# Block 0 of a network of residual blocks on one core: one mask transfer a slot, two key buffers, one product to divide heads, the maxima's rows copied by ScalarE, a norm in one piece ahead of the keys

## The reference

```python
def _attn(q, k, v, mask):
    scores = jnp.einsum('bqhd,bkhd->bhqk', q, k) / np.float32(np.sqrt(HD))
    scores = jnp.where(mask[:, None, None, :], jnp.float32(-jnp.inf), scores)
    w = jax.nn.softmax(scores, axis=-1)
    return jnp.einsum('bhqk,bkhd->bqhd', w, v)
```

## Time and profile before

| | |
|---|---|
| median of 3 runs | 5856.54 us (5856.24 to 5871.77) |
| the profiled execution | 5850.62 us, span 5848.7 us |
| busy: TensorE, its weight load | 5394.6, 4270.3 us |
| busy: VectorE, ScalarE, GpSimd | 4044.0, 3144.3, 2240.2 us |
| mean granted clock of TensorE | 0.961 of full speed |
| block 0 | from about 60 to 2960 us of the span |

### The profile page before, as it was taken

How to read it: one execution, slowest core, us unless ns; L and a number is a source line. 1 busy time by engine, 2 the same in 40 slices (tenths; PEclk the granted TensorE clock), 3 DMA queues, 4 the chain that set the end, 5 groups by cost and what they waited for, 6 DMA issues and landing times.

```text
span 5848.7 us, 144909 instructions
## 1 busy us (share of the span) xinstructions
PE 5394.6 (92%) x57797; PEld 4270.3 (73%) x57797; DVE 4044.0 (69%) x8355; ACT 3144.3 (54%) x6405; POOL 2240.2 (38%) x2209
## 2 busy tenths in 40 slices
PE   5899999999999999999978999999699999989998
PEld 4667677676776766767645799998389889947984
DVE  3888887888888888888744377776556666644653
ACT  1566666766666667666644333434334334424764
POOL 4665665666666666666500000000011111075440
PEclk8999999999999999999988999999899999998998
DMA  2776776767767777677810011110100000030000
GB/s 63 118 124 100 122 116 108 122 110 117 120 110 120 112 114 123 103 124 116 119 51 20 22 33 33 38 37 13 41 12 12 17 17 12 12 121 11 2 1 26
DMA packets 440503, 408.12 MB, mean 70 GB/s; under 512 B 125576, under 2 KB 420947, under 8 KB 437787
## 3 DMA queue, kind: packets, MB, share of 16 engines
q1 hardware_dynamic: 439834, 398.85, 39.2%
HBM read 158.00 MB, written 0.46 MB: 27 GB/s over the span
## 4 chain that ended last, share of the span: by engine, by line
PE 61%; POOL 8%; DVE 7%; SPq 7%; issue 6%; DMA 5%; ACT 4%; POOLq 1%; DVEq 1%; ACTq 0%
PE psum L2248 10%; PE psum L2278 10%; PE psum L1575 5%; PE psum L1587 4%; PE psum L1561 4%; SPq L1475 3%; POOL slot_context L3547 3%; DMA l_ctx_v<-in_ctxV 3%; PE psum L1609 3%; PE psum L1723 3%; PE psum L1601 2%; PE psum L416 2%; SPq L1493 2%; PE psum L430 2%; DVE row_max L1940 2%
## 5 line engine op out<-in xcount | busy, mean ns | idle before, releaser
L1940 DVE TENSOR_REDUCE row_max<-psum 112x1 f32<-112x500 f32 x2304 | 1443.5, 670 | 187.4 <-PE psum L1575 172.6
L2067 ACT ACTIVATE weights<-psum 125x448 f32<-125x448 f32 x2304 | 1141.3, 541 | 521.7 <-PE psum L1561 515.2
L1575 PE MATMUL psum<-key_stack,query_stack 97*128 97x500 bf16 x2304 | 875.7, 381 | 107.9 <-DMA query_stack<-query_parts 47.9
L1561 PEld LDWEIGHTS psum<-query_stack,key_stack 121*128 121x128 bf16 x9216 | 654.6, 99 | 370.7 <-issue 184.4
L1561 PE MATMUL psum<-query_stack,key_stack 121*128 121x112 bf16 x9216 | 837.9, 213 | 33.5 <-ACT weights L2067 28.0
L2278 PE MATMUL psum<-l_ctx_v,l_weights 125*128 125x129 f32 x5376 | 638.6, 274 | 1.8 <-ACT l_u L2352 1.8
L2278 PEld LDWEIGHTS psum<-l_ctx_v,l_weights 125*128 125x128 f32 x5376 | 618.3, 191 | 2.5 <-issue 2.5
L1587 PE MATMUL psum<-weights,values 125*17 125x112 f32 x18432 | 554.9, 261 | 0.0
L1587 PEld LDWEIGHTS psum<-weights,values 125*17 125x17 f32 x18432 | 408.9, 97 | 144.8 <-issue 140.4
L2097 POOL TENSOR_TENSOR key_parts<-key_temp,key_parts 128x500 bf16<-128x500 f32 x288 | 327.2, 1136 | 421.5 <-ACT key_parts L1970 421.5
L2087 POOL TENSOR_TENSOR key_temp<-key_temp,rope_sin 128x500 f32<-128x500 f32 x288 | 360.5, 1252 | 282.2 <-DVE key_temp L1821 282.2
(11 more groups left out here) (549 smaller groups left out, 10227.5 us busy)
## 6 DMA issues: line engine op xcount, KB each, us to landing
key_stack<-key_parts SPq DMA_DIRECT2D x1728, 125.0 KB, 4.6
ctx_t<-in_ctxT SPq DMA_DIRECT2D x96, 750.0 KB
l_ctx_v<-in_ctxV SPq DMA_DIRECT2D x32, 750.0 KB
query_stack<-query_parts SPq DMA_DIRECT2D x576, 28.0 KB, 3.4
l_ctx_t<-in_ctxT SPq DMA_DIRECT2D x16, 750.0 KB
slot_context<-in_ctxV SPq DMA_DIRECT2D x16, 750.0 KB
key_stack<-ctx_mask_rows SPq DMA_DIRECT2D x576, 3.9 KB
sm_w<-in_sm_w SPq DMA_DIRECT2D x3, 2048.0 KB
```

Source lines behind the costliest of these rows:

```text
L1561: mm = e.matmul(self.k.psum[:, h, (p % 4) * QC:(p % 4 + 1) * QC], ks[:, at:at + 128], q[:, p * QC:(p + 1) * QC])
L1575: e.matmul(self.k.psum[:, 2 + n % 2, 0:500], q[0:ROWS_MAX, p * QC:p * QC + 128], ks[0:ROWS_MAX, p, c * 500:(c + 1) * 500]).then_inc(self.m ...
L1940: e.tensor_reduce(self.largest[:, i % PAIRS, i // PAIRS:i // PAIRS + 1], k.psum[0:QC, 2 + i % 2, 0:500], AX.X, ALU.max, negate=True).then_ ...
L2067: e.activation(half(self.p[kt % RING_P], h), self.k.psum[0:KN, h, 0:HALF], ACT.Exp).then_inc(self.exped.sem, 1)
```

## The change

1. The mask of the context is held as one row of 1500 for each batch (16 partitions) instead of six of 250, and SP stacks it with one transfer a slot instead of six.
2. `key_temp` becomes two buffers, taken in turn, so VectorE waits for the last part of the block before the last.
3. The transposed sums' pieces are placed 8 columns lower for odd ones, so that all heads lie 32 columns apart and `divide` needs one product instead of four.
4. The rows are copied by ScalarE (`rows_scalar`), at the top of step 11, ahead of the exponentials of that step.
5. GpSimd applies both halves of a norm in one step, and does so ahead of its query and key work of that step.

```diff
-            self.mask_rows = sb("ctx_mask_rows", [6 * B, L // 6], BF16)[:, :]
+            self.mask_rows = sb("ctx_mask_rows", [B, L], BF16)[:, :]
...
-            for n in range(6):
-                e.dma_start(dst[ROWS:ROWS + 1, :, n * 250:(n + 1) * 250],
-                            self.mask_rows[6 * b + n:6 * b + n + 1, :].unsqueeze(1).broadcast_to(
-                                [1, PAIRS, 250])).then_inc(self.mask_stacked.sem, 16)
+            e.dma_start(dst[ROWS:ROWS + 1, :, :],
+                        self.mask_rows[b:b + 1, :].unsqueeze(1).broadcast_to([1, PAIRS, L])).then_inc(
+                            self.mask_stacked.sem, 16)
...
             for i in range(4):
-                tr = e.transpose(side.bank(*key)[0:S, i * 128:(i + 1) * 128], self.acc[:, i * S:(i + 1) * S],
-                                 k.ident[:, :])
+                at = i * 128 - 8 * (i % 2)
+                tr = e.transpose(side.bank(*key)[0:S, at:at + 128], self.acc[:, i * S:(i + 1) * S], k.ident[:, :])
...
-        for g in range(2):
-            for h2 in range(2):
-                v = blocks[:, g, 128 * h2:128 * (h2 + 1)].rearrange("p (j c) -> p j c", j=4)[:, :, 1 + 8 * h2:9 + 8 * h2]
-                m = 2 * g + h2
-                op = e.tensor_tensor(o[:, m * 32:(m + 1) * 32].rearrange("p (j d) -> p j d", j=4), v,
-                                     spread(inv[:, 4 * m:4 * m + 4], 8), ALU.mult)
-        op.then_inc(side.emptied(*key), 1)
+        e.tensor_tensor(o.rearrange("p (m d) -> p m d", d=8), bk.rearrange("p (m c) -> p m c", c=32)[:, :, 1:9],
+                        spread(inv, 8), ALU.mult).then_inc(side.emptied(*key), 1)
...
-            if (b, c) > (0, 0):
-                e.wait_ge(self.key_lo.sem, self.key_lo(b, c) - 1)
-            bk = side.bank(*key)[:, 0:500]
-            e.stream_shuffle(self.tm[:, 1, :], bk, OTHER_HALF).then_inc(self.key_turned.sem, 1)
+            if (b, c) > (0, 1):
+                e.wait_ge(self.key_lo.sem, self.key_lo(b, c) - 2)
+            bk, tm = side.bank(*key)[:, 0:500], self.tm[(3 * b + c) % 2]
+            e.stream_shuffle(tm[:, 1, :], bk, OTHER_HALF).then_inc(self.key_turned.sem, 1)
...
-    def rows_vector(self, e, b):
+    def rows_scalar(self, e, b):
...
-        e.tensor_copy(self.q_stack[b % 3][ROWS:ROWS_ALL, :].rearrange("r (p c) -> r p c", p=PAIRS),
-                      rows.unsqueeze(1).broadcast_to([1 + 3 * PAIRS, PAIRS, QC])).then_inc(self.side.emptied(*key), 1)
+        e.activation(self.q_stack[b % 3][ROWS:ROWS_ALL, :].rearrange("r (p c) -> r p c", p=PAIRS),
+                     rows.unsqueeze(1).broadcast_to([1 + 3 * PAIRS, PAIRS, QC]), ACT.Copy).then_inc(
+                         self.side.emptied(*key), 1)
...
         for s in self.slots():
             for kt in range(KT):
+                if 0 <= s + 1 < NS and kt == 11:
+                    self.rows_scalar(e, s + 1)
                 for h in range(2 if 0 <= s < NS else 0):
...
+                ph, t = s // BH, 12 * (s % BH) + kt
+                for name, at in T_NORM.items():
+                    layer = MLP_OF(ph) if name == "mlp" else NEXT_OF(ph)
+                    if layer is not None and t == at + 3:
+                        for h in range(2):
+                            self.norm_gpsimd(e, name, ph, layer, h)
                 if 0 <= s + 2 < NS:
                     self.query_gpsimd(e, s, kt)
                 self.key_gpsimd(e, s, kt)
-                ph, t = s // BH, 12 * (s % BH) + kt
-                for name, at in T_NORM.items():
-                    layer = MLP_OF(ph) if name == "mlp" else NEXT_OF(ph)
-                    if layer is not None and t - at - 3 in range(2):
-                        self.norm_gpsimd(e, name, ph, layer, t - at - 3)
```

More of the change, by code:

```diff
@@ L1290, in __init__ @@
             self.q_tmp = sb("query_block", [128, 2, QC])
-            self.tm = sb("key_temp", [128, 2, 500])
+            self.tm = [sb(f"key_temp{i}", [128, 2, 500]) for i in range(2)]
             self.ctx_t = [sb(f"ctx_t{i}", [128, L])[:, :] for i in range(2)]
@@ L1313, in __init__ @@
                 self.src_mask8 = k.sb(s2, "src_mask8", [1, T], U8)[:, :]
-                self.ctx_mask8 = k.sb(s2, "ctx_mask8", [6 * B, L // 6], U8)[:, :]
+                self.ctx_mask8 = k.sb(s2, "ctx_mask8", [B, L], U8)[:, :]
         self.tables_arrived = ev("l0_tables_arrived", step=112)
@@ L1328, in __init__ @@
         self.part_stacked = [ev(f"key_part{i}_stacked", NS * 3 // 2, step=16 * len(K_PARTS)) for i in range(2)]
-        self.mask_stacked = ev("key_mask_stacked", NS, step=96)
+        self.mask_stacked = ev("key_mask_stacked", NS, step=16)
         self.q_stacked = [ev(f"query_stack{i}_arrived", NS // 3, step=16 * len(Q_PARTS)) for i in range(3)]
@@ L1509, in sync @@
         e.dma_start(self.parity, dr["head_parity"]).then_inc(sem, 16)
-        e.dma_start(self.ctx_mask8, dr["ctx_mask"]).then_inc(sem, 16)
+        e.dma_start(self.ctx_mask8, dr["ctx_mask"].rearrange("(b n) c -> b (n c)", b=B)).then_inc(sem, 16)
         e.dma_start(self.bias[:, :, :], dr["l0_bias"]).then_inc(sem, 16)
@@ L1739, in phase_tensor @@
                 for m in range(4):
-                    tr = e.transpose(side.bank(*key)[0:S, m * 128:(m + 1) * 128], self.sacc[:, m * S:(m + 1) * S],
-                                     k.ident[:, :])
+                    at = m * 128 - 8 * (m % 2)
+                    tr = e.transpose(side.bank(*key)[0:S, at:at + 128], self.sacc[:, m * S:(m + 1) * S], k.ident[:, :])
                 tr.then_inc(side.filled, 1)
@@ L1817, in fixed_vector @@
             e.wait_ge(side.filled, side.at(*key))
-            if (b, c) > (0, 0):
-                e.wait_ge(self.key_lo.sem, self.key_lo(b, c) - 1)
-            bk = side.bank(*key)[:, 0:500]
-            e.stream_shuffle(self.tm[:, 1, :], bk, OTHER_HALF).then_inc(self.key_turned.sem, 1)
-            e.tensor_tensor(self.tm[:, 0, :], bk, self.cos[:, cols], ALU.mult).then_inc(side.emptied(*key), 1)
+            if (b, c) > (0, 1):
+                e.wait_ge(self.key_lo.sem, self.key_lo(b, c) - 2)
+            bk, tm = side.bank(*key)[:, 0:500], self.tm[(3 * b + c) % 2]
+            e.stream_shuffle(tm[:, 1, :], bk, OTHER_HALF).then_inc(self.key_turned.sem, 1)
+            e.tensor_tensor(tm[:, 0, :], bk, self.cos[:, cols], ALU.mult).then_inc(side.emptied(*key), 1)
         if 1 <= s <= NS and kt == 2:
@@ L1933, in vector @@
                     self.max_parts_vector(e, s + 1)
-                if 0 <= s + 1 < NS and kt == 11:
-                    self.rows_vector(e, s + 1)
                 if self.max_at(s, kt):
@@ L2074, in key_gpsimd @@
     def key_gpsimd(self, e, s, kt):
-        tm, side = self.tm, self.side
+        side = self.side
         for late in range(1, 4):
@@ L2083, in key_gpsimd @@
             b, c = at
-            part = self.k_part[(3 * b + c) % 2]
+            part, tm = self.k_part[(3 * b + c) % 2], self.tm[(3 * b + c) % 2]
             if late == 1:
```

9 lines of the change are left out of this document (4 added, 5 removed).

## The result

The changed kernel took 5882.96 us in the median against 5853.44 for the kernel before: 1.0047 times, 95% interval 1.0039 to 1.0054, some 27 us slower. The forecast was 5885. The experiments took it apart.

The account below looks back on a forecast made before the run. TensorE, busy 477.68 of 500 us, was taken as the bound. The terms summed to +31 us on the profiled 5850.62, so 5882, or 5887 as a median; the forecast was put at 5885, range 5840 to 5925.

Parts of the forecast that it names:

- Wait behind the MLP's norm: Step 9, eleven slots: GpSimd's norm delays the key and ScalarE's key copy, TensorE stands 4.2 each; +46 us.
- The clock behind it: TensorE's granted clock falls behind each of these eleven long waits, 2.0 us each; +22 us, bounds 0 to 37.
- The first rival: The wait is there, but TensorE's clock holds or other waits give it back: +9, 5865 us; chance 0.17.
- Self and cross norms and two buffers: Remainders 1 and 5: VectorE's 0.32 wait for the last key part goes, 0.33 in 22 places; -7 us.
- Rows on ScalarE: Rows' copy: -18 us from TensorE's waits behind remainders 2 to 4, +7 from 0.25 in 27 light slots.
- Mask: SP's five fewer issues a slot shorten TensorE's waits for queries: -15 us, and -5 for the clock.
- Divide: One product instead of four saves VectorE 0.4 in 184 places, hidden by TensorE; 5 us at best, no loss.
- Start: Ahead of the first self attention: +2 us for the masks' longer conversion, less 1 for the first slot's queries.
- The sum: All terms together: 46 + 22 + 7 + 1 - 7 - 18 - 15 - 5 = +31 us.
- The signs named in advance: Profile after: ScalarE's key copy and TensorE wait about 4 us eleven times, half clock behind, query waits 25 to 35, maxima's waits up.
- The third rival: ScalarE is not held behind the MLP's norm, as the roots come early enough: -37, 5820 us; chance 0.13.
- The second: TensorE's waits for queries go whole, all 47.9 us and eight stretches at lower clock: -11, 5846 us; chance 0.10.

Follow-up runs that it names:

- b_mask_only: The kernel before with one mask transfer a slot instead of six and nothing else changed: 5828.16 us, ratio 0.9960.
- a_norm_old: The changed kernel with the norm's part undone whole, every norm in halves behind the keys: 5829.34 us, ratio 0.9960.
- the first experiment: The changed kernel with the MLP's norm alone put behind the key again, half in step 9 and half in step 10: 5811.05 us.
- b_norm_only: The kernel before with only both halves of every norm in one step, ahead of the keys: 5975.25 us, ratio 1.0199.
- the half dose: The changed kernel with the first half of the MLP's norm ahead of the key and the second half behind it: 5853.4 us.

## Why the prediction was right, point by point

- **Wait behind the MLP's norm**, 46: right, and the mechanism was seen as forecast. One wait is 4.86 in slot 48, not 4.2. The norm and key took 6.43 against 6.38, and started 0.10 later behind the roots; the rows' copy pushes back by 0.10 more than the 0.82 I took; from the pair of exponentials to TensorE it is 0.69, not 0.49, as I counted no signal; and TensorE gets there 0.19 earlier. That is 0.64. Against the kernel without the hold it is 4.34 a time, 48 in all, since 0.58 of the step would be there by the rows' copy anyway.
- **The clock behind it**, 22: 23 by the account. The 2.0 for one were 2.1. The first rival, that the clock holds, falls.
- **Self and cross norms and two buffers**, -7: the buffer gave 9, by the very 0.33 named. That the norm ahead gives nothing by itself since VectorE's rotation is next was right too: 8.57 stays 8.57. The step that failed is that I costed it beside the kernel before: in company with ScalarE's copy it gives 22 us, because the copy makes ScalarE last there. Costing two buffers at nothing beyond the 7 left out that they are the condition of the norm's part: without them it costs 52 us more (117 against 65).
- **Rows on ScalarE**, -18 + 7: wrong by 39 us as a part alone (+28). The gain's places were right: the five steps behind remainder 2 to 4 are 0.36 to 0.49 shorter, and the 7.8 are gone. The cost was mis-placed and mis-sized: 0.58 in each light slot, not 0.25 (27 times, 16 us, not 7), and 1.05 in step 11 of 22 slots behind the self and cross norms, where ScalarE had a wait of 3.13 and thus no lead. Behind the cross norm half or less of that 1.05 stays by the end of the next slot's step 1 (8.73 to 9.08 against 8.57). Most of the error in the light slots can be named from the rows of slot 47. TensorE starts 0.69 behind the pair of exponentials (1608.20 to 1608.89), of which I counted 0.49 for the first, so 0.20 is left for the signal and not 0.1. The copy pushes back by 0.93 (1607.27 to 1608.20) and not 0.82. The prediction's own sum then gives 0.93 + 0.20 - 0.68 = 0.45. On top came 20 us of clock and 20 of waits for queries. Taken out of the changed kernel, though, the same part is worth -8 (error 9), which the forecast's -11 fits. Which term one calls wrong depends on the company in which it is measured.
- **Mask**, -15 - 5: -14 and -9 in block 0, -23 in all. The waits' part was right to a us or two, the list's 29.5 to 32.2 lie in the 25 to 35 named. In the last slot the lateness is gone as read: the second key block's issue starts at 2950.11, 0.02 behind its last part. The wait is not so simply the smaller of two numbers. It went from 2.91 to 1.52 in the changed kernel, 1.39 of the 1.6 to gain, but to 2.14 with the mask's part alone, 0.77 of them. SP's issues are not of one length either: the six of that key block took 3.88 in the kernel before, 4.34 and 5.05 in these two. SP and TensorE in the changed kernel, then TensorE in b_mask_only:

```profile
2947.11 0.70 SPq L1482 DMA_DIRECT2D key_stack<-ctx_mask_rows  x1
2950.11 4.34 SPq L1475 DMA_DIRECT2D key_stack<-key_parts  x6
```

```profile
2961.03 0.39 PE L1574 MATMUL psum<-key_stack,query_stack 97*128 97x500 bf16 x1 [1.52 <-DMA query_stack<-query_parts]
```

```profile
2905.96 0.38 PE L1574 MATMUL psum<-key_stack,query_stack 97*128 97x500 bf16 x1 [2.14 <-DMA query_stack<-query_parts]
```

- **Divide**, 0: not to be told from none.
- **Start**, +2 - 1: the masks' conversion takes 3.98 us against the 3.9 forecast, but the first scores of slot 0 come at 178.9 before and 178.0 after, and between 176.7 and 184.7 in the other kernels. No run here can tell a term of 1 us from none.
- **The sum.** With the norm's part taken out of the changed kernel and the other four put alone into the kernel before it is 73 - 22 - 9 + 28 - 23 - 3 = +44 against +27 measured. (With the norm's part put in alone too it would be 117 - 9 + 28 - 23 - 3 = +110: the parts don't add.) The 17 left over are by the medians no larger than their error, but the waits of block 0 (one execution each) show the same more clearly: -14, -2, +30 and +3.5 alone make +17.5, and the four together (a_norm_old) make -11. The wait for queries shows most of it: 47.9 before, 67.6 with the rows' copy alone, 29.5 with one mask transfer alone, and 30.5 with both and the others (a_norm_old). The same wait is 54.1 with the divide part alone, so it moves by some 6 by itself. That the copy delays ScalarE and so what SP waits for, and that SP has room for it with five issues fewer, is argued and not shown. So my two errors, 24 us of gain too little for the self and cross norms with the buffers and, with this, some 22 of cost too little for the rows, cancelled; the sum was right by its large terms and by that luck.
- **The signs named in advance.** All held: the maxima's waits, forecast up behind the rotations, are up there (0.56 to 0.79), though down in total, from 33.4 (53 times) in the same list of the kernel before to 23.5.
- The third rival (ScalarE not held) is out by the first experiment. The second (queries' waits go whole) is out: they went by a third.

The Trainium skill (VectorE: DVE Perf Modes, Mode 2×_1P) had been weighed for whether ScalarE would double on the 16-bit rows. The trace after answers for this shape: 896 bf16 columns take 905 ns on ScalarE, what the 0.82 ns a column of its fp32 rows gave (0.91), as against 618 on VectorE. There is no doubling; the page, which states the packing of VectorE, is not contradicted.

```profile
L1830 ACT ACTIVATE query_stack<-psum 25x896 bf16<-25x896 bf16 x88 | 79.7, 905 | 2.2
```

## What to carry to other kernels

On an engine that serves two consumers in a fixed order, put first the work whose reader is next in the chain of the bound, and ask of a piece of work put ahead not only how long it runs but how long it waits for its own input with the engine blocked: here 1.2 us of idle with the key at hand, and 3.8 of norm, stood ahead of a 2.6 us key. Cost the parts of a change in the company of each other: the same copy was +28 us in one kernel and -25 in the next, and a buffer worth 9 alone was worth 60 beside a reordering. Where an engine has lead only in some rounds of a pattern, give it the extra work in these rounds alone.

## What was not expected of the hardware

- The granted clock fell during TensorE's wait of 4.86, not behind it (0.78 over two us without a matmul, then 0.51), and how much of the lower stretch falls on work decides its price: 2.1 of 6.8 us.
- The same wait of 1.95 us has half clock behind it in one slot and full clock in another, and of the waits of 3.0 in the half dose only some. The clock's loss in block 0 went from 1.9 to 62.6 us over fourteen kernels, one execution of each. It made up 9 of the 21 us by which block 0 got shorter with the mask's part, and 20 of the 34 by which it got longer with the rows'. What decides a single case is left open.
- The rest of block 0 is some 4 to 15 us lower where ScalarE copies the rows (2605 to 2613 against 2617 to 2623, but for b_norm_only, 2609). Which short gaps these are was not followed up.
